# Attention scores issued one at a time, a maxima score of one head beside an exponentials score of the other, with the values between the two halves of a slot

## What is computed

```python
x = x + attn(layernorm(x))                      # all 8 sequences, full softmax over 512 keys
q, k, v = heads(x @ Wq), heads(x @ Wk), heads(x @ Wv)
att = where(causal, q @ k.T * scale, -inf)
y = softmax(att) @ v                            # causal
attc = qc @ kc.T * scale
y = y + softmax(attc) @ vc                      # cross, 512 keys
x = x + (y @ Wp + bp)
x = x + moe(layernorm(x))                       # argmax gate, capacity 256 per expert
```

## Time and profile before

| what | us |
|---|---|
| median of 3 runs | 1753.51 (1742.24 to 1759.99) |
| the profiled execution | 1735.63 |
| its span, first to last instruction | 1733.8 |
| PE busy | 1465.2 (85%) |
| DVE busy | 1275.1 (74%) |
| ACT busy | 1036.8 (60%) |
| POOL busy | 496.3 (29%) |

### The profile page before, as it was taken

The page is one execution under the profiler, slowest core; times in us unless marked ns, Lnnn a source line. Parts: engine busy times, 40 slices in busy tenths (PEclk is TensorE's granted clock), DMA queues, the critical chain, the costliest instruction groups (busy, mean ns, idle before and its releaser), DMA issues.

```text
span 1733.8 us, 37922 instructions
## 1 busy us (share of the span) xinstructions
PE 1465.2 (85%) x14699; PEld 661.2 (38%) x14699; DVE 1275.1 (74%) x2610; ACT 1036.8 (60%) x2086; POOL 496.3 (29%) x350
## 2 busy tenths in 40 slices
PE   3268988889889988889889889898898888769997
PEld 1122333233223343433424334334343332249997
DVE  2377887787778787787887877878878778337775
ACT  1137767766766757666566666665665656515553
POOL 3344434534510110202213113012140221324554
PEclk9679999999999999999999999999999998889999
DMA  2714333442432234332343143323331332238771
GB/s 89 200 45 120 100 101 108 102 103 94 107 84 54 64 83 93 74 67 87 82 103 79 53 99 99 74 73 85 101 85 54 88 71 98 72 114 275 262 258 64
DMA packets 119095, 176.22 MB, mean 102 GB/s; under 512 B 25505, under 2 KB 85511, under 8 KB 114312
## 3 DMA queue, kind: packets, MB, share of 16 engines
q1 hardware_dynamic: 110992, 158.89, 34.3%
q0 software_dynamic: 5888, 14.24, 2.5%
q10 hardware_dynamic: 2048, 0.83, 0.2%
HBM read 102.72 MB, written 51.18 MB: 89 GB/s over the span
## 4 chain that ended last, share of the span: by engine, by line
PE 46%; DVE 25%; DMA 7%; POOL 6%; issue 6%; SPq 4%; ACT 4%; ACTq 0%; POOLq 0%; DVEq 0%
DVE negmax L1048 15%; PE psO L634 10%; PE psM L404 9%; PE psS L657 7%; PE psK L404 6%; PE psK L689 4%; PE psS L404 4%; DMA shared<-shared 4%; ACT probs L896 3%; DMA stack<-mrows 2%; DVE parts L1109 2%; POOL shared L1295 2%; POOL shared L1298 2%; DVE stats L996 2%; PE psM L722 1%
## 5 line engine op out<-in xcount | busy, mean ns | idle before, releaser
L1048 DVE TENSOR_REDUCE negmax<-psS 128x1 f32<-128x512 f32 (+3 forms) x1536 | 868.0, 615 | 233.8 <-PE psS L657 134.0
L896 ACT ACTIVATE probs<-psK 128x512 f32<-128x512 f32 (+3 forms) x1536 | 753.3, 544 | 396.9 <-PE psK L689 243.7
L634 PE MATMUL psO<-probs,V 128*32 128x256 f32 (+1 forms) x5632 | 444.1, 387 | 28.3 <-ACT U L888 23.3
L657 PE MATMUL psS<-stack 48*128 48x512 f16 (+3 forms) x1536 | 285.3, 368 | 89.5 <-DVE negmax L1048 73.8
L689 PE MATMUL psK<-stack 50*128 50x512 f16 (+3 forms) x1536 | 278.6, 359 | 19.4 <-DMA stack<-mrows 15.7
L657 PEld LDWEIGHTS psS<-stack 48*128 48x128 f16 x1536 | 74.4, 93 | 412.9 <-DVE negmax L1048 309.9
L634 PEld LDWEIGHTS psO<-probs,V 128*32 128x32 f32 x5632 | 113.3, 108 | 216.3 <-issue 146.3
L1274 POOL TENSOR_TENSOR shared<-packed,recipB 128x1024 f32<-128x1024 f32 x8 | 18.9, 2360 | 370.3 <-DMA recipB<-recip_scratch 370.3
L1253 POOL TENSOR_TENSOR rstd<-lnt,minus_half 128x4 f32<-128x4 f32 x24 | 24.7, 1028 | 238.3 <-DVE lnt L1012 238.3
L689 PEld LDWEIGHTS psK<-stack 50*128 50x128 f16 x1536 | 76.4, 95 | 41.6 <-issue 13.0
L589 PE MATMUL psK<-wo 128*128 128x512 f16 x304 | 83.3, 394 | 0.6
(11 more groups left out here) (157 smaller groups left out, 1923.1 us busy)
## 6 DMA issues: line engine op xcount, KB each, us to landing
spare<-in_L_ffn_w_dram SPq DMA_DIRECT2D x32, 1024.0 KB, 6.4
parts_scratch<-parts SPq DMA_DIRECT2D x192, 128.0 KB
stack<-parts_scratch SPq DMA_DIRECT2D x96, 256.0 KB, 6.8
stack<-parts_scratch SPq DMA_DIRECT2D x96, 128.0 KB, 4.3
packed<-U SPq DMA_DIRECT2D x192, 64.0 KB
recipB<-recip_scratch SPq DMA_DIRECT2D x48, 256.0 KB
shared<-shared SPq DMA_DIRECT2D x64, 128.0 KB, 2.5
probs<-back_scratch POOLq DMA_DIRECT2D x16, 258.0 KB, 3.2
```

What stands on the lines that cost most here:

```text
L634: mm = nc.tensor.matmul(psO[32 * i:32 * i + 32, q0:q1], v_of(par)[:, kt, 2 * g + i % 2 + PAIRS * (i // 2), :], probs[:, (unit + i % 2) % P ...
L657: mm = nc.tensor.matmul(psS[:, banks[hh], 0:n], stack_of(par, 0)[rows, hp, qt * P:(qt + 1) * P], stack_of(par, 1)[rows, hp, 0:n], start=Tr ...
L896: nc.scalar.activation(probs[:, t % P_RING, i, q0:T], psK[:, S_BANKS[t][i], q0:T], ACT.Exp, scale=SM_SCALE / (1 if b.kind == "A" else WSCA ...
L1048: nc.vector.tensor_reduce(negmax[:, g % 2, at:at + 1], psS[:, S_BANKS[u // 2][j], 0:n], AX_X, ALU.max, negate=True).then_inc(s["max_done"], 1)
```

## The change

On PE a slot becomes: `scores(0)`, `values()`, `scores(1)`, then warm-up and job as before. `scores(i)` issues the maxima score of head i and right behind it the exponentials score of head 1 - i. The two use different halves of the array's rows, so that they can run side by side as two maxima scores did. Their masks in kind B are interleaved. Banks are taken in rotation (`s_bank`, `k_bank`), one at a time: a maxima score waits for `max_done` k - 2, an exponentials score for `exp_done` 2t + i - 2. ACT takes the heads in the order in which they come (`1 - i`). Waits of ACT and DVE, jobs and all DMAs stay as they were. The number of matmuls and their sizes are the same.

```diff
-S_BANKS = ((1, 2), (0, 1), (2, 0)) * 10 + ((1, 2), (1, 0))
...
+        def s_bank(b, later, u):
+            return (b.n + later + u) % RING_S
+        def k_bank(b, t, i):
+            return (b.n + 2 * t + i) % RING_K
...
-                    def maxima():
...
-                        need(pe, s["max_done"], b.at("max_done", k - 1))
...
-                        for hh in range(2):
-                            rows = slice(PART * hh, PART * hh + STACK)
-                            mm = nc.tensor.matmul(psS[:, banks[hh], 0:n], stack_of(par, 0)[rows, hp, qt * P:(qt + 1) * P],
...
-                    def exponents():
...
-                        need(pe, s["exp_done"], b.at("exp_done", w - 1))
-                        if t == 0:
-                            keep_warm(psK[:, banks[0], :], b.warm_rows)
...
+                    def scores(i):
+                        later, u, k = s_unit(b, t, i)
+                        kind = has_s(b, later)
+                        if kind:
...
+                            need(pe, s["max_done"], b.at("max_done", k - 2))
+                            n = (qt + 1) * P if kind == "B" else T
+                            out_q, rows = psS[:, s_bank(b, later, u), :], slice(PART * i, PART * i + STACK)
...
+                            mm = nc.tensor.matmul(out_q[:, 0:n], stack_of(par, 0)[rows, hp_q, qt * P:(qt + 1) * P],
...
+                        if b.kind:
+                            g, kt, hh = t // 8, t % 8 // 2, 1 - i
+                            need(pe, s["exp_done"], b.at("exp_done", 2 * t + i - 2))
+                            out_k = psK[:, k_bank(b, t, i), :]
+                            if t == 0 and i == 0:
+                                keep_warm(out_k, b.warm_rows)
+                            if t % 8 == 0 and i == 0:
+                                pe.wait_ge(s[f"negmax_in_{g % 2}"], b.at(f"negmax_in_{g % 2}", (0, 32, 32, 64)[g]))
...
+                            mm = nc.tensor.matmul(out_k[:, q0:T], stack_of(b.parity, 1)[rows, hp, kt * P:(kt + 1) * P],
...
-                    maxima()
-                    exponents()
+                    scores(0)
+                    values()
+                    scores(1)
...
-                            nc.scalar.activation(probs[:, t % P_RING, i, q0:T], psK[:, S_BANKS[t][i], q0:T], ACT.Exp,
+                            nc.scalar.activation(probs[:, t % P_RING, 1 - i, q0:T], psK[:, k_bank(b, t, i), q0:T], ACT.Exp,
...
-                        nc.vector.tensor_reduce(negmax[:, g % 2, at:at + 1], psS[:, S_BANKS[u // 2][j], 0:n], AX_X, ALU.max,
+                        nc.vector.tensor_reduce(negmax[:, g % 2, at:at + 1], psS[:, s_bank(b, later, u), 0:n], AX_X, ALU.max,
```

More of the change, by code:

```diff
@@ L619, in _, with values @@
                 for t in range(SLOTS):
-                    av = b.av(t)
-                    if av:
+                    def values():
+                        av = b.av(t)
+                        if not av:
+                            return
                         prev, unit, q0, q1, first = av
@@ L661, in maxima @@
                                 mm.then_inc(s["scores_q"], 1)
[L662 to L671, removed]
@@ L692, in exponents @@
                             if b.kind != "B":
                                 mm.then_inc(s["scores_k"], 1)
+                        if kind == "B":
+                            nc.tensor.matmul(out_q[:, n - P:n], unit_a[all_q, :], mask_q[all_q, :], start=False, stop=False,
+                                             skip_group_check=True)
                         if b.kind == "B":
[L695 to L698, removed]
@@ L699, in exponents @@
-                            for hh in range(2):
-                                rows = slice(PART * hh, PART * (hh + 1))
-                                mm = nc.tensor.matmul(psK[:, banks[hh], q0:q0 + P], unit_b[rows, :], mask_k[rows, :], start=False,
-                                                      stop=True, skip_group_check=True)
-                                mm.then_inc(s["scores_k"], 1)
-                    maxima()
-                    exponents()
+                            nc.tensor.matmul(out_k[:, q0:q0 + PART], unit_a[all_k, :], mask_k[all_k, PART:P], start=False, stop=False,
+                                             skip_group_check=True)
@@ new lines, in scores @@
+                        if kind == "B":
+                            mm = nc.tensor.matmul(out_q[:, n - PART:n], unit_b[all_q, :], mask_q[all_q, 0:PART], start=False, stop=True,
+                                                  skip_group_check=True)
+                            mm.then_inc(s["scores_q"], 1)
+                        if b.kind == "B":
+                            mm = nc.tensor.matmul(out_k[:, q0:q0 + P], unit_b[all_k, :], mask_k[all_k, :], start=False, stop=True,
+                                                  skip_group_check=True)
+                            mm.then_inc(s["scores_k"], 1)
```

40 lines of the change are left out of this document (14 added, 26 removed).

## The result

The changed kernel takes 1770.14 us in the median of 20 runs (1753.51 to 1785.06), the kernel before 1745.13 us (20 runs). The ratio is 1.011, with a 95% interval of 1.008 to 1.014: slower by 1.1%. Medians in this document are over all runs, ratios and intervals over the fast ones alone, since a few runs fell in a slower state. The profiled execution has a span of 1766.0 us, against 1733.8. The forecast was +1.15%.

What follows compares the result with a forecast made beforehand. PE was taken to lead (busy 85% of the span), with DVE having its share. Costs of 64 us less savings of 27 and 17 gave +20 us, 1774 us on the median's scale; the range ran from 1735 to 1825.

Steps and rivals of the forecast that it cites:

- part 1: On PE, job slots make four tile-shape changes, not three, at 0.09 us each: +20 us in kinds B and C, +3 in A.
- part 2: In kind B, a narrow score beside a wide one waits for it, twice per slot: +27 us.
- a sign of being wrong: Narrow head's masks beside the wide score at no cost, DVE idle well under 199 us and a faster run.
- part 3: At every eighth slot, values and the second half now stand behind PE's wait for the maxima rows' DMA: +11 us.
- part 4: In even slots ACT's exponentials start later, since the values they wait for now stand behind the first half: +3 us.
- parts 5 and 6: On PE, maxima wait less for DVE's reduces, -27 us, and jobs wait less for DVE to empty psM, -17 us.
- part 5: On PE, max_done is asked for k - 2, one bank at a time, so maxima wait less for reduces: -27 us.
- Cancelling: First rival: PE's waits absorb or give up enough that added and saved cancel, sum +2 us, time 1755; chance 0.28.
- The second rival: Finer steps feed DVE more evenly and nearly all of 104 us of PE's waits goes: -24 us, time 1729; chance 0.20.
- The third: Rival: a wait for exp_done between a half's two matmuls breaks pairs, one in eight: +62 us in all, time 1815; chance 0.10.

Runs made afterwards that it cites:

- the first experiment's repeat: The group-start experiment measured again in the third set against the kernel before: 1735.26 us, ratio 0.9976.
- the version with the values first: The changed kernel with values ahead of both mixed halves at every eighth slot only; 1724.0 us, ratio 0.987 to the kernel before.
- The eight buffers: The group-start experiment with eight probs buffers, not four, and ACT's wait for values moved back four slots; 1743.43 us, ratio 0.9989 to the kernel before.
- the group-start experiment: The changed kernel, but at every eighth slot both maxima scores, then values, then both exponentials scores; first set 1760.0 us, ratio 0.986 to the kernel before.
- the run with more shape changes: The group-start experiment plus one tiny matmul at 318 places, two tile-shape changes each; 1755.31 us, ratio 1.0067 to the kernel before.

## Why the prediction was right, point by point

The time (+1.15% forecast, 1.1% measured) and the sign were right. No term had the wrong sign, but the sizes were off: costs of 64 us and savings of 44 were forecast, and both came out smaller in the time. That the difference fits so closely is partly luck.

**Shape changes (part 1, +23 us): too large.** The step is as forecast, 0.09 us, and there is one more in a job slot. But only a quarter of such work is seen in the time. By that rate it makes 339 x 0.09 / 4 = 8 us, an estimate. The forecast took PE's added work in kinds B and C at its full price.

**Unequal widths (part 2, +27 us): too large.** The narrow masks run beside the wide score, and the next half's score starts on the free rows. This was named as a sign of being wrong, together with a faster run; it came without one. In the time nothing shows when unequal widths are taken out of kind B together with the mixing, and undisturbed B bodies are only 0.3 to 1.2 us longer.

**Group starts (part 3, +11 us): too small, and the heart of the matter.** They cost about 24 us by the first experiment's repeat, 13 in kinds B and C and the rest in kind A, and 40 by the version with the values first. The forecast counted the waits that were there before (20) and had few others join. In fact most of the starts had little slack: 59 waits were seen, and over the whole attention those in kinds B and C went from 6 to 42. The work that the order put behind the wait was what had covered the DMA. This is the term that was too small, by a factor of two to four. It also left out that the clock falls in a long wait (last section), and that in kind B the first maxima score is not finished ahead of the wait. The second cannot weigh much: the version with the values first shares it and is the fastest of all.

**ScalarE (part 4, +3): not contradicted.** The eight buffers show no cost in the order of the group-start experiment, where these waits were 93.5 us. With the 214.9 of the changed kernel it was not tried.

**Savings (parts 5 and 6, -27 and -17): right in kind.** Waits for reduces fell by 42.5 us and those for `psM` by 18 in the five rows, both beyond the forecast. How much reached the time isn't measured by itself. A wait that gets shorter need not be a saving, since added work shortens waits too: the run with more shape changes took 38 us out of them and was slower. If the other terms are 8, 0 and 24 us, 13 of the 44 us of savings are left for the measured 19 us, and 29 if the group starts are 40; this is arithmetic, not a run. The version with values first at group starts, which keeps these savings, is 1.3% faster than before, so the mixed halves are worth something once the group starts are right. With the old order and the one-bank waits alone the time hardly moves (0.9974), so the bank rule by itself isn't what helps, against part 5, which put the saving on it.

**The rivals.** Cancelling would have been within 1%, the measurement is just above it; its interval reaches down to 0.8%. The second rival, a faster kernel by finer steps, is what the change becomes when its group starts are mended. The third, pairs broken by a late exponential, shows in the trace at 38 places, or 59 by the starts; the pairs at the group starts are broken by the DMA, which is part 3 and not this rival.

## What to carry to other kernels

Where one engine issues a wait in program order, count what stands behind it and not only how long it was before: a reordering that does no harm elsewhere can take the cover off a DMA wait that recurs every few slots. Put the work that needs nothing ahead of it, at those places alone. And before a change is given up for a loss of 1%, look which wait has grown; here the order in 96 of 768 slots turned +1.1% into -1.3% in one and the same set of runs.

## What the runs showed that was not expected

The clock adds to the price of a wait. Summed from 115 us to the last exponentials, PE ran at 1.2 GHz for 55 us in the kernel before (12 stretches), for 121 us in the changed one (24 stretches), 116 in its repeat, 88 with values first at group starts and 85 in the repeated group-start experiment. Half of 66 us more is 33 us of speed at most, out of the 85 us by which PE's busy time grew. Stretches like the one after 396 us come with long waits for the maxima rows (3.85, 4.49 and 4.51 us), and others with shorter ones (2.06 us at 205).

The repeat of the change and that of the group-start experiment, traces of two sets, show how the 24 us may divide. Their attention differs by 27 us: PE's idle time by 13, its busy time by 14, and half of the 31 us less at 1.2 GHz is 15. By this, about half is the wait itself and about half the slower clock behind it.

It is not a matter of single traces. The mean granted clock over all runs is 0.944 in the change (26 runs, two sets), 0.964 in the kernel before (55 runs in the second and third set), 0.966 with values first at group starts (6) and 0.958 in the repeated group-start experiment (12). What was given away, at most, is one minus that, times the run's time: 98 us in the change, 63 in the kernel before, 59 with values first. The 39 us between the first and the last is as large as the 40 us between their times. No run holds the clock and the order apart, so how much of it is cause is not shown.

Work added to PE, which leads the chain of the kernel before with 46%, was seen at a quarter of its size, in a kernel whose waits could absorb it. The share of the chain is no measure of what a little more work there costs.

The ratio of two kernels can differ between sets of runs by more than its interval: the same pair gave 0.986 (0.983 to 0.989) in the set where the kernel before took 1783 us and 0.998 (0.995 to 1.000) in the one where it took 1742.
